# The adjacency in transfers of 2 MB into three double slots, instead of 1 MB into six single ones

## Time and profile before

| | us |
|---|---|
| median of 3 runs | 3223.37 |
| lowest, highest | 3218.17, 3226.78 |
| the profiled execution, its own time | 3221.74 |
| its span, first to last instruction | 3219.9 |

### The profile page before, as it was taken

How to read it: one execution, slowest core, us unless ns; L and a number is a source line. 1 busy time by engine, 2 the same in 40 slices (tenths; PEclk the granted TensorE clock), 3 DMA queues, 4 the chain that set the end, 5 groups by cost and what they waited for, 6 DMA issues and landing times.

```text
span 3219.9 us, 36379 instructions
## 1 busy us (share of the span) xinstructions
PE 3068.0 (95%) x14003; PEld 2294.9 (71%) x14066; DVE 2867.5 (89%) x2458; ACT 2321.4 (72%) x1556; POOL 17.1 (1%) x39
## 2 busy tenths in 40 slices
PE   6999999999999999999998999988888999999998
PEld 5888888788778887788876788767666555555554
DVE  6877787778799888999899999999999999999997
ACT  4666666766677677876777767766776788888886
POOL 2000000000000000000000000000000000000000
PEclk8999999999999999999999999999999999999999
DMA  9888788888899999999999999988999999999996
GB/s 331 338 345 310 296 330 318 323 309 334 320 371 398 380 369 388 385 399 369 378 385 355 364 374 378 376 320 324 370 375 379 377 375 383 383 384 380 384 389 242
DMA packets 159898, 1150.26 MB, mean 357 GB/s; under 512 B 18016, under 2 KB 18208, under 8 KB 20400
## 3 DMA queue, kind: packets, MB, share of 16 engines
q1 hardware_dynamic: 157968, 1143.15, 90.9%
q0 software_dynamic: 608, 2.69, 0.4%
q10 hardware_dynamic: 1152, 2.10, 0.2%
HBM read 1145.77 MB, written 2.10 MB: 356 GB/s over the span
## 4 chain that ended last, share of the span: by engine, by line
PE 75%; DVE 20%; issue 3%; DMA 2%; ACT 1%; SPq 0%; DVEq 0%; ACTq 0%
PE ACC L781 32%; PE ACC L788 17%; DVE lo L538 13%; PE ACC L890 13%; PE PSF L904 4%; PE PST L904 3%; DMA raw<-in_at 1%; PE PSF L847 1%; DVE SV L654 1%; DMA O<-in_x_rows 1%; PE PST L819 1%; PE PST L793 1%; DVE M L553 1%; PE PSF L845 1%; DVE SV L661 1%
## 5 line engine op out<-in xcount | busy, mean ns | idle before, releaser
L399 ACT CAST hi<-raw 128x2048 fp32r<-128x2048 f32 x832 | 1585.9, 1913 | 677.6 <-PE ACC L781 507.7
L538 DVE TENSOR_TENSOR lo<-raw,hi 128x2048 fp32r<-128x2048 f32 x832 | 1879.2, 2288 | 197.3 <-ACT hi L399 193.5
L781 PE MATMUL ACC<-hi,T 128*128 128x512 f32 x5568 | 1422.4, 395 | 13.5 <-POOL T L388 11.8
L781 PEld LDWEIGHTS ACC<-hi,T 128*128 128x128 f32 x5568 | 1051.7, 190 | 250.0 <-issue 18.7
L788 PE MATMUL ACC<-lo,T 128*128 128x512 f32 x3200 | 882.0, 398 | 102.5 <-DVE lo L538 101.0
L788 PEld LDWEIGHTS ACC<-lo,T 128*128 128x128 f32 x3200 | 605.2, 191 | 259.0 <-DVE lo L538 134.9
L405 ACT ACTIVATE Wf<-ACC,w_bias 128x1024 fp32r<-128x1024 f32 x512 | 568.4, 1114 | 132.0 <-PE ACC L890 131.8
L553 DVE SCALAR_TENSOR_TENSOR M<-raw,M 128x512 bf16<-128x512 f32 x1008 | 629.6, 689 | 31.4 <-PE ACC L890 18.8
L890 PE MATMUL ACC<-M,rank_b 128*128 128x512 bf16 x1969 | 517.1, 381 | 11.4 <-ACT Wf L405 5.6
L890 PEld LDWEIGHTS ACC<-M,rank_b 128*128 128x128 bf16 x2032 | 158.6, 98 | 264.6 <-issue 124.3
L904 PE MATMUL PST<-Wf,S 128*128 128x512 f32 x512 | 208.4, 488 | 0.0
(11 more groups left out here) (139 smaller groups left out, 1029.8 us busy)
## 6 DMA issues: line engine op xcount, KB each, us to landing
raw<-in_at SPq DMA_DIRECT2D x1088, 1024.0 KB, 6.1
O<-in_x_rows SPq DMA_DIRECT2D x8, 256.0 KB, 5.1
SV<-in_x_cols POOLq DMA_DIRECT2D x1, 2048.0 KB, 19.8
out<-O ACTq DMA_DIRECT2D x8, 256.0 KB, 2.4
bias<-in_bias_rows SPq DMA_DIRECT2D x1, 128.0 KB, 2.9
l1w_sb<-in_l_w POOLq DMA_DIRECT2D x2, 64.0 KB, 6.7
rank_f<-in_rank_mats POOLq DMA_DIRECT2D x1, 128.0 KB, 8.1
w_sb<-in_w POOLq DMA_DIRECT2D x2, 64.0 KB, 9.4
```

Source lines behind the costliest of these rows:

```text
L399: nc.scalar.copy(hi[:, c % NH], raw[:, c % NR]).then_inc(hi_done, 1)
L538: tt(lo[:, c % NR], raw[:, c % NR], hi[:, c % NH].bitcast(f32), ALU.subtract).then_inc(lo_done, 1)
L781: ins = mm(acc[:, part], w, hi[:, p.c % NH, s, part], start=p.opens and s == 0 and i == 0, stop=False)
```

## The change

A transfer now brings two neighbouring pairs, c even and c + 1: 2 MB, 16 KB together to a partition. The host's layout has them side by side, so that each partition's 16 KB are one run in memory. The buffer raw keeps its size and place; it is used as three double slots, with three semaphores. SP issues only at even c, and waits before it for pair c - 5, the second pair of the double slot's last use, where before it waited for c - 6 ahead of c and for c - 5 ahead of c + 1. ACT and DVE wait for the whole double slot before they touch either half. In the rank stage, where chunks are read backwards, the first pair of two is the upper half of the double slot. NR, NH, the table of steps, and all work on PE, ACT and DVE are as before.

```diff
-    raw_in = [sem(f"raw_in{s}") for s in range(NR)]
+    raw_in = [sem(f"raw_in{s}") for s in range(NR // 2)]
...
+    def slot(c):
+        return c // 2 % (NR // 2) * 2 + (c % 2 if c < n_pairs else 1 - c % 2)
+
+    def arrived(eng, c):
+        eng.wait_ge(raw_in[c // 2 % (NR // 2)], 16 * (c // NR + 1))
...
-                s, before = c % NR, c - NR
+                if c % 2:
+                    continue
+                before = c - NR + 1
                 if 0 <= before < n_pairs:
                     sp.wait_ge(pair_done, before + 1)
...
-                sp.dma_start(raw[:, s], at[(I * NB + J) * NP + pr].rearrange(
-                    "p (s i) -> p s i", s=2)).then_inc(raw_in[s], 16)
+                t = c // 2 % (NR // 2)
+                sp.dma_start(raw[:, 2 * t:2 * t + 2], at[((I * NB + J) * NP + pr) // 2].rearrange(
+                    "p (t s i) -> p t s i", t=2, s=2)).then_inc(raw_in[t], 16)
...
-                act.wait_ge(raw_in[c % NR], 16 * (c // NR + 1))
+                arrived(act, c)
...
-                    dve.wait_ge(raw_in[c % NR], 16 * (c // NR + 1))
+                    arrived(dve, c)
...
-        "at": c(adj.reshape(NB, BLK, NB, 4, Q // 4, P).transpose(0, 2, 3, 5, 4, 1)).reshape(
-            NB * NB * 4, P, (Q // 4) * BLK),
+        "at": c(adj.reshape(NB, BLK, NB, 2, Q // 2, P).transpose(0, 2, 3, 5, 4, 1)).reshape(
+            NB * NB * 2, P, (Q // 2) * BLK),
```

More of the change, by code:

```diff
@@ L398, in split_hi @@
                     act.wait_ge(lo_done, c - NH + 1)
-                nc.scalar.copy(hi[:, c % NH], raw[:, c % NR]).then_inc(hi_done, 1)
+                nc.scalar.copy(hi[:, c % NH], raw[:, slot(c)]).then_inc(hi_done, 1)
             def weights(m):
@@ L537, in split_lo @@
                 dve.wait_ge(hi_done, c + 1)
-                tt(lo[:, c % NR], raw[:, c % NR], hi[:, c % NH].bitcast(f32), ALU.subtract).then_inc(lo_done, 1)
+                tt(lo[:, slot(c)], raw[:, slot(c)], hi[:, c % NH].bitcast(f32), ALU.subtract).then_inc(lo_done, 1)
             def count(m):
@@ L547, in count @@
                     part = slice(h * HALF, (h + 1) * HALF)
-                    src = raw[:, c % NR, 1 - m % 2, part]
+                    src = raw[:, slot(c), 1 - m % 2, part]
                     if m % G == 0:
@@ L787, in multiply @@
                         part = slice(h * HALF, (h + 1) * HALF)
-                        ins = mm(acc[:, part], ws[s][0], lo[:, p.c % NR, s, part], start=False, stop=p.closes and s == 1)
+                        ins = mm(acc[:, part], ws[s][0], lo[:, slot(p.c), s, part], start=False, stop=p.closes and s == 1)
                 ins.then_inc(pair_done, 1)
```

## The result

The changed kernel takes 3438.43 us (median of 4 runs, 3433.39 to 3444.94) against 3222.26 us before (4 runs): ratio 1.0668, 95% interval 1.0654 to 1.0681. It is 216 us slower. The forecast was 3269 us, 46 more than before, in a range from 3226 to 3305: the sign was right, the size was off by a factor of more than four. The profiled execution has a span of 3432.4 us, 212.5 more than before.

The account below looks back on a forecast made before the run. The prediction took PE (75% of the chain) and DVE (20%) as the bound, with DMA nearly hidden. It added 4.5 + 35.5 + 6 = 46 us to the profiled 3221.74, giving 3267.7, or 3269 as median; range 3226 to 3305.

Parts of the forecast that it names:

- The landing, 7.4 us: Every double transfer: 4.9 us for the first MB plus 2.49 for the second, 7.4 from issue; bounds 7.1 and 9.8.
- 26 places: Places, DVE-bound or at steps at PE's pace, where a late even pair costs time; 3 us less landing put at 8 us.
- the cover at the even pace, 0.9 us: At PE's 2.72 us a pair, lo would still end 0.9 us before PE wants it, so 0 us lost.
- The first sweep, 0 us: From 100 to 800 us: DVE's waits of up to 7.1 us for PE's small products swallow delays; 0 us lost.
- The DVE-bound stretches, 35.5 us: Where DVE is the busy engine, late lo is lost at once: 42.6 us, less 7.1 of existing waits, leaves 35.5.
- the three steps: DVE's steps at PE's pace, at 1870, 1926 and 1993 us, where PE loses time to a late lo: 4.5 us.
- The 23 places: Even pairs in four DVE-bound stretches from 880 to 2490 us where a new delay is added: 42.6 us before deduction.
- The start, 6 us: Blocks of x queue behind 2 MB instead of 1 and land 2.5 us later: 6 us, bounds 0 and 17.
- The rank stage, 0 us: From 2490 us on: a double slot is needed 10.8 us after it is asked for, against 7.4 landing; 0 us lost.
- Hidden anyway: Whole kernel: most local delays are caught up before the next step, no change, about 3227 us; chance 0.16.
- faster: Whole kernel: larger transfers lift the queue's rate and shorten ACT's waits for data, about 3205 us; chance 0.12.
- The far rival: Whole kernel: a double transfer is not pipelined, lands after 9.8 us and breaks PE's even pace, about 3380 us; chance 0.10.

Follow-up runs that it names:

- The two runs with comb moved: PE's small products of the first sweep moved behind the odd pair: in the changed kernel 3426.33 us, in the kernel before 3235.34 us.
- The two runs with one coarse wait each: Kernel before with single slots: issuing two pairs' transfers together after pair c - 5, 3268.63 us; waiting for both pairs' data at even pairs, 3259.57 us.
- The half-bytes run: Changed kernel with its waits and double slots, but from pair 6 on each transfer brings only the first MB of its two: 3231.42 us.
- the wait for both: Kernel before with its issue times, but at an even pair ACT (DVE in the rank stage) also waits for the neighbour's MB: 3259.57 us.
- the two kernels of the start: Kernel before with blocks of x issued one step earlier, 3223.31 us; the same with the 2 MB load of x's columns in eight pieces, 3216.10 us.

## Why the prediction was wrong

**The step that failed: what a late pair has in hand.** The direction, the mechanism (data asked for at c - 5 and coming with its neighbour's) and the rank stage were right. What was wrong is the amount lost for each late pair, in three terms, and a little at the start.

*The landing, 7.4 us.* It was made from 4.9 in light load and 2.49 for the second MB. Measured: never under 7.5 in that stretch, 8.0 in its median, 8.9 at PE's even pace. The light-load value was put into stretches that are loaded, though the trace of before showed medians of 6.6 and maxima of 8.5 in such a one. The range had a slip that hid how much hangs on this: it puts 3 us of landing over 26 places at 8 us, which is the value for 0.3 us; 3 us would be 78. I had written that the cover at the even pace, 0.9 us, is gone at a landing of 8.3. The median there is beyond it, so pairs 320 to 399 and 448 to 543 lost 26 us instead of 0. There one late double slot looks like this: its issue, hi, lo and PE's matmuls (timeline of the changed kernel, one engine each).

```profile
1638.46 0.33 SPq L373 DMA_DIRECT2D raw<-in_at  x1
1648.09 3.72 ACT L409 CAST hi<-raw 128x2048 fp32r<-128x2048 f32 x2 [4.07 <-DMA raw<-in_at]
1650.03 4.49 DVE L548 TENSOR_TENSOR lo<-raw,hi 128x2048 fp32r<-128x2048 f32 x2 [3.30 <-ACT hi L409]
1650.05 2.11 PE L791 MATMUL ACC<-hi,T 128*128 128x512 f32 x8 [0.71 <-ACT hi L409]
```

The data of both comes 9.6 us after the issue; ACT stands idle for 4.07 us, DVE for 3.30 and PE for 0.71. The next two slots were 9.5 and 9.3 us on their way, ACT waited 1.61 and 1.55 us for them, and PE did not wait at all. Before, ACT waited there for PE, 82 times, and for data 7 times.

*The first sweep, 0 us.* I saw that DVE waits in each block of rows for PE's small products, and took this wait for cover. It is one of the causes. Those products stand, as step comb, between an even pair and the odd one. Before, the transfer of pair 136 was released by pair 130 and left at 448.36, ahead of them; only 137 had to wait for their end:

```profile
448.36 0.33 SPq L363 DMA_DIRECT2D raw<-in_at  x1
458.61 0.33 SPq L363 DMA_DIRECT2D raw<-in_at  x1
```

Now both wait for pair 131. The data of 136 is there at 499.18, ACT's root stands behind hi of that pair, DVE's step behind the root and lo of 136 behind the step; so PE, five pairs after the products, waits for DVE (ACT, DVE and PE of the changed kernel, pair 136):

```profile
499.18 1.91 ACT L409 CAST hi<-raw 128x2048 fp32r<-128x2048 f32 x1 [5.18 <-DMA raw<-in_at]
504.68 4.49 DVE L548 TENSOR_TENSOR lo<-raw,hi 128x2048 fp32r<-128x2048 f32 x2
507.01 2.07 PE L798 MATMUL ACC<-lo,T 128*128 128x512 f32 x4 [3.70 <-DVE lo L548]
```

The issue was at 490.2, landing 9.0 us later. A block of 32 pairs took 103.1 to 108.0 us before, and 107.3 to 116.7 now. The block shown is the longest, and part of it is the clock: the products of this block ran at full clock before, and from 478.4 on at half clock now (busy PE, PEld, DVE, ACT, POOL; PE clock, DMA share, GB/s; first before, then changed):

```profile
448.20:455.60 7.40, 7.40 (x66) 7.28 (x65) 3.12 (x2) 1.21 (x1) 0.00 (x0) 1.00 0.60 231
478.40:488.70 10.30, 10.30 (x44) 9.72 (x44) 5.75 (x7) 0.60 (x1) 0.00 (x0) 0.50 0.09 38
```

From the end of pair 130 to that of 131 it was 10.3 us before and 15.1 now. The two runs with comb moved show the mechanism for about two fifths of the 48 us.

*The DVE-bound stretches, 35.5 us, with the three steps 40.* They lost 125. The 23 places were counted one at a time, each with the distance that the trace of before showed, and I let the existing waits swallow 7 us. I think that once DVE has stood, PE's steps, the root on ACT and the release of slots shift against each other, and the next slot is late from another cause; this is argued, not shown place by place. In the last sweep the count gave 14 us after that deduction; DVE's wait for hi there (2065 to 2487 before, 2214 to 2697 after) went from 6.3 us to 62.0. That growth of 55.7 us is nearly all of the stretch's loss of 60.2:

```profile
DVE lo L538 <- ACT hi L399: 6.3, 13, 1.7
```

```profile
DVE lo L548 <- ACT hi L409: 62.0, 49, 4.7
```

The wait for data that I said would swallow 7.1 us grew ninefold instead. The two runs with one coarse wait each (+43 and +34, against +173 together) say the same for the whole: the costs of places that draw on the same distance are not to be added from the schedule of before.

*The start, 6 us.* 9.9 measured. Block 1 landed at 18.7 instead of 29.8, so pair 1 was done 12 us earlier, which I had not seen; the blocks after it ate this up (DVE waited 9.5 us for block 2) and 10 more.

*The rank stage, 0 us,* was right although its landing was not 7.4: the median is 9.7 for the transfers issued from 2720 to 3300. It was the 10.8 us in hand that held, as the prediction had said for a landing of 9.8.

**The rivals.** Hidden anyway and faster are both out: no even pair's data came in less than 7.4 us. The Trainium skill, "DMA: Bandwidth & Descriptors", section "Anatomy of one DMA — SWDGE (gpsimd) path", has a fit by which 2 MB would take an estimated 6.8 us. The same page of the Trainium skill, section "Measured (HBM→SBUF, 128 partitions, SWDGE, issued from GpSimd)", asks for transfers of 1 MB or more. Here, on SyncE's queue, 2 MB took 7.4 to 11.2 us when issued after the first 110 us, and the rule, which is about the rate of the queue, did not help a kernel that is bound by when the data comes. The far rival, 3380 us, was the nearest to the truth, to which I gave 0.10. Its landing of 9.8 was too long for the median, but its two terms, PE's even pace broken and each place dearer, are what happened. It too had them too small: 40 to 60 us for the pace, where 75 were lost, and 60 more for the places, where it was 85 more than the forecast.

**What stays open.** The clock granted to PE is 0.91 in the last sweep against 0.94 before, and 0.972 against 0.980 in the whole; PE's busy time rose by 89 us with the same instructions. The half-bytes run has 0.981. The prediction had named a lower clock as a sign against it, unpriced. The two means bound its direct share: 0.020 of 3219.9 us is 64 us of full-speed time not granted before, 0.028 of 3432.4 is 96 now, so at most some 32 of the 212 us. How much of this is an effect of the longer gaps I did not separate. Why waits for data of 390 us cost 9 us in one run and others of 415 cost 34 is argued from the distances, not shown place by place; by stages the difference is mostly in the last sweep, which took 422.1 us with half the bytes, 439.9 with the wait for both and 425.2 before.

## What to carry to other kernels

Before slots are merged, count for the loaded state, not the idle one: time from the release that now triggers the transfer to its landing, against the time until the first consumer needs it, and look at what stands between the two merged releases on the releasing engine. Where a pipeline has little distance to spare (one slot less cost 64 us here, most of it where DVE is the bound), two coarsenings that cost 34 and 43 us alone can cost 173 together; the sum of single delays is then far too low. To learn whether a wait or the time behind it is to blame, keep the waits and cut the bytes: one run of this kind told more here than the others together, although it takes load off the queue as well. And before two traces are compared stage by stage, compare the granted clock in each stage: here a block of rows came out 5 us longer or shorter by that alone.

## What the runs showed of the hardware

A transfer of 2 MB to 128 partitions lands 7.4 us after its issue at the least with rows of 16 KB and 7.3 us with rows of 8 KB, one of 1 MB after 4.6 us. What the rows add under load depends on the stretch: medians of 8.9 and 7.6 us from 1380 to 1640 and from 1400 to 1600, but 8.8 and 8.8 from 2214 to 2697.

A 256 KB load with 2 KB rows, issued at 3.6 us behind 4 MB of its own queue, landed after 26.2 us while a 2 MB load with 32 KB rows from another queue was in flight. In the two kernels of the start a block of x stood behind 4 MB too, issued at 4.35 and 4.16 us: it landed after 29.9 us with the large load whole, and after 16.9 us where that load was cut into eight pieces that began at 21.8 us. A block issued before any of the adjacency, right behind another block of x, landed after 4.4 us.

The granted clock fell to 0.5 during PE's small products in some blocks of rows and stayed at 1.0 in others of the same execution, with PE busy throughout: 4 of these matmuls with 64 columns took 0.61 us at 1.0 and 1.06 us at 0.5.
